# Moving every attention product to VectorE in a hand-ordered two-layer kernel, with more filler matmuls and the order laid anew

## The chip, the cores and the metric

The kernel runs on one core of a Trainium2 chip. The metric is the device time of one execution in microseconds (us). Before the change three runs took 551.32, 551.1 and 556.45 us, with a median of 551.32.

## The reference, cut to what is computed

The input is x (4 batches x 512 positions x 128 channels) and a context of 77 keys per batch. All arithmetic is fp32. Four residual blocks follow one another:

```python
x = x + xattn0(layernorm(x), ctx, ctx, mask, Wq, bq, Wk, bk, Wv, bv, Wo, bo)    # 16 heads x 8, 77 keys, softmax
x = x + ffn0(layernorm(x), ...)
#   ffn0: y1 = LN(z + mha(z))      sequence axis = the 4 batches, 4 heads x 32: scores are 4x4 for each position and head
#         y2 = LN(y1 + moe(y1))    top-1 of 8 experts, each (y1 @ w1 + b1) @ w2 + b2, at most 256 tokens each, times the gate
x = x + xattn1(layernorm(x), ctx)  # q = z Wq^T, k = ctx Wk^T, v = ctx, 16 heads x 8
#         cutoff = the 32nd largest of the 77 scores; scores below it are left out; softmax over the rest
x = x + mix(layernorm(x))          # sigmoid(xr W_r) * (relu(xk W_k)^2 W_v), xr and xk mix each position with the one before it
```

The expert layers have no nonlinearity between w1 and w2, so the kernel multiplies the two weights once at the start.

## The kernel before, in words

**Tiles.** The 2048 positions are 16 tiles of 128 positions (partitions) by 128 channels, t = 4b + j for batch b and quarter j. The first cross-attention (`attend`) runs in four groups j of four tiles; `s0@2` is its score step for b = 0 in group 2. The small attention over the batches (`among`) needs the four tiles of one j together and also runs once for each j. The expert layer, the second cross-attention and the channel mix run tile by tile, t = 0 to 15.

**The order of the work.** Each step of a stage is one token, name@index, in a table ORDER that is written out by hand. Each engine walks the table from front to back and issues those steps that it has a function for (`run`); what order it keeps is that of the table, and semaphores alone tie the engines together. A token such as `norm@3` may stand for a piece on one engine, and the pieces of a tile's chain stand apart in the table with other tiles' work between them. Some wait values are counted from the table (`begun`), so they follow a new order by themselves.

**The first cross-attention.** TensorE makes the scores of 16 heads (s0 to s3, L1070 and L1073), VectorE takes the maximum (mx, L726) and subtracts it (sub, L731), ScalarE exponentiates (exp), TensorE turns the weights (ta, tb, tc), ScalarE copies them (ca, cb, cc, L516 among them), TensorE multiplies with the values (v0 to v3, L1102, 20 matmuls or 10 of two passes), VectorE normalises (nm), TensorE turns and projects (ot, op, L1113), and VectorE adds the residual (x0 to x3, L747). The merging of the expert weights (wa0 to wa7, wt, wu) is TensorE work put among the steps of groups 0 and 1.

**The attention over the batches.** VectorE stores q, k and v (qs, L814). Four products follow, one for each query batch l: qk{l} multiplies q of l with the k of all four (128x512). dot{l} sums them (L845), soft, mexp (L556 on ScalarE) and softw make the softmax, four weighted products wv{l} multiply the values with the weights, and tot{l} sums them (L871). Before the change VectorE makes qk0, qk1 (L821) and wv0, wv1, wv2 (L830); POOL makes qk2, qk3 (L369) and wv3 (L378). The constants QKG = 2 and WVG = 3 set that split, and POOL signals by semaphores of its own:

```python
if l < QKG:
    hold(e, s["m_prod"], QKG * j + l + 1)
else:
    hold(e, s["m_prodg"], (B - QKG) * j + l - QKG + 1)
```

POOL also adds biases (zbias L345, xbias L350), copies the gates (L407), makes the scalars of the layer norms (L395, L397, L399), applies their affine part (L411, L415) and, for each tile of the second attention, makes the difference to the maximum (dif, L430), the difference to the cutoff (cut, L437) and the masked weights (product, p, L444).

**The expert layer.** For each tile: turn and copy, then three matmul steps moe0 to moe2 (L1239), each followed by ScalarE's gated copies (gated0 to gated2: L595, then eight of L598, 3, 4 and 1), then a sum of nine on TensorE (total, L1247), and the layer norm (sum2, square2 L574, scale2 on POOL, norm2 L579, affine on POOL, and sum3 to norm3 again). `cap` is POOL's step that prepares the gates of one group, which the expert tiles of a later j need.

**The second cross-attention.** lturn, lT, ask, qT and scores make the 16 x 77 scores in PSUM; keep (ScalarE, L626) copies them to SBUF; VectorE then finds the 32nd largest by four rounds of maxima of eight (max{round}{head group}, L959) with three rounds of marking the found ones (mark, L967) between them. The 16 tiles follow each other on VectorE without an end, 16 heads x 7 steps each. exp (L634) and sign (L638, L640) on ScalarE and product on POOL make the weights; turn0 to turn2 (L1283) with copy0 to copy2 (L648 to L652) turn them; value (L1299, 20 matmuls) multiplies with the context; norm (VectorE, L992 and L995) normalises. The last tile, 15, is split up by head groups (part0 to part3) and value0 to value2. Then come the channel mix of that tile: fturn, shift, up, acts, down (L1326), fvalue, half and end, and the store.

**Fillers.** `fill@k` is two bf16 matmuls of 128x308 into the half of the turning PSUM that the channel mix also uses (psT[:, 1], L1331); nobody reads the result. They stand where TensorE would otherwise idle. `stoke@k` is the same into the last bank of the score PSUM, free once the last scores are copied. Before the change there are 157 fills and 10 stokes; each of the stokes also waits for a step of the last tile's top-k:

```python
def after():
    hold(e, s["S_kept"], NT)
    hold(e, s["topk_step"], TOPK_STEPS * NT - (STOKES - (k - FILLS)) + 1)
    stream(psS[:, G - 1])
```

## Time and profile before

| what | value |
|---|---|
| runs | 551.32, 551.1, 556.45 us (median 551.32) |
| the profiled execution | 555.6 us |
| its span, first to last instruction | 553.8 us |
| TensorE's mean granted clock in it | 0.88 of full speed |
| VectorE busy | 481.4 us |
| TensorE busy (matmul) | 431.9 us |
| ScalarE busy | 291.3 us |
| GpSimd (POOL) busy | 277.4 us |

All durations below come from the one profiled execution, which took 4.3 us more than the median of the runs. The span is what the trace covers; 1.8 us of the execution lie outside it. Busy shares are means over stages of different kinds: to about 75 us cross-attention with TensorE full, to about 300 us a mixture of all stages, then tile after tile of top-k. Which engine or wait ends a stretch is read from the stretch.

In the rows PE is TensorE's matmul and PEld its weight load, DVE is VectorE, ACT is ScalarE, POOL is GpSimd. Bracketed at a row's end is the time that the engine stood idle before it, and what ended that.

### The profile page before, as it was taken

The numbers are of one execution on the slowest core, as the hardware profiler recorded it, in microseconds if no ns is written. First come the engines' busy times: TensorE is split into PE (matmuls) and PEld (weight loads), VectorE is DVE, ScalarE is ACT, GpSimd is POOL, SyncE is SP. The second block draws the span as 40 slices with busy tenths as digits, with TensorE's granted clock in tenths as the row PEclk, the third lists the DMA queues.
The fourth block names the chain that finished last, engine by engine and source line by source line (L and its number), as shares of the span: only waits on it lengthen the run. The fifth ranks groups of instructions, "written<-read, shape, count | busy, mean of one in ns | idle before, by whom it ended". The sixth has DMA issues, their size and how long they took to land. (4 is left out here: it accounts for less than half of the span.)

```text
span 553.8 us, 10801 instructions
## 1 busy us (share of the span) xinstructions
PE 431.9 (78%) x2655; PEld 325.0 (59%) x2655; DVE 481.4 (87%) x3014; ACT 291.3 (53%) x797; POOL 277.4 (50%) x400
## 2 busy tenths in 40 slices
PE   4989997797896886878977987877876976765285
PEld 4569865566655663656655655655654754553274
DVE  4954679959868798999899999999999999999971
ACT  1225551323443435424877688787777687544333
POOL 4410141504327447535575578668648567554612
PEclk9999998978996999899989899878778889556768
DMA  9600000000000000000000000000000000000000
GB/s 279 290 1 1 2 1 1 1 2 0 2 2 0 2 2 0 2 0 2 7 6 2 5 2 2 11 1 1 11 1 7 1 7 6 2 10 2 5 5 11
DMA packets 5933, 9.60 MB, mean 17 GB/s; under 512 B 744, under 2 KB 4976, under 8 KB 5616
## 3 DMA queue, kind: packets, MB, share of 16 engines
q1 hardware_dynamic: 5584, 8.35, 4.3%
q10 hardware_dynamic: 288, 0.56, 0.3%
q8 instruction: 23, 0.38, 0.3%
q14 instruction: 38, 0.31, 0.2%
HBM read 7.86 MB, written 1.05 MB: 16 GB/s over the span
## 5 line engine op out<-in xcount | busy, mean ns | idle before, releaser
L959 DVE MAX8 top<-area_b 128x8 f32<-128x77 f32 x768 | 112.8, 222 | 0.0
L967 DVE MATCH_REPLACE8 area_b<-top,area_b 128x77 f32<-128x77 f32 x512 | 106.9, 222 | 0.0
L1283 PE MATMUL psT<-consts,p 128*128 128x128 f32 (+1 forms) x160 | 35.1, 348 | 33.8 <-POOL p L444 27.0
L1331 PE MATMUL psT<-mrow,mones 128*128 128x308 bf16 x314 | 53.3, 309 | 1.4 <-ACT pT L516 0.8
L967 DVE MATCH_REPLACE8 area_b<-top,area_a 128x77 f32<-128x77 f32 x256 | 53.5, 223 | 0.0
L1299 PE MATMUL psM<-vblk,pT 128*128 128x135 f32 (+3 forms) x320 | 48.8, 316 | 3.2 <-ACT pT L652 2.6
L1299 PEld LDWEIGHTS psM<-vblk,pT 128*128 128x128 f32 (+1 forms) x320 | 46.5, 225 | 7.6 <-issue 7.2
L1102 PE MATMUL psM<-vblk,pT 128*128 128x135 f32 (+3 forms) x320 | 44.2, 296 | 7.8 <-ACT early L579 4.5
L1283 PEld LDWEIGHTS psT<-consts,p 128*128 128x128 f32 (+1 forms) x160 | 23.1, 174 | 44.4 <-POOL p L444 29.4
L1102 PEld LDWEIGHTS psM<-vblk,pT 128*128 128x128 f32 (+1 forms) x320 | 41.4, 204 | 11.3 <-issue 9.8
L598 ACT ACTIVATE mparts<-psM,cur 128x128 f32<-128x128 f32 x128 | 38.1, 368 | 9.4 <-PE psM L1239 9.3
L444 POOL TENSOR_TENSOR p<-area_b 128x1232 f32<-128x1232 f32 x15 | 41.8, 2787 | 2.0 <-ACT area_b L640 0.9
L1331 PEld LDWEIGHTS psT<-mrow,mones 128*128 128x128 bf16 x314 | 31.8, 103 | 17.9 <-issue 8.5
L959 DVE MAX8 top<-area_a 128x8 f32<-128x77 f32 x256 | 37.5, 223 | 3.6 <-ACT area_a L626 3.6
L967 DVE MATCH_VALUE_LOAD area_b<-top,area_b 128x8 f32 x512 | 40.6, 79 | 0.0
L1247 PE MATMUL psM<-mparts,consts 128*128 128x128 f32 x288 | 39.9, 300 | 0.0
L1247 PEld LDWEIGHTS psM<-mparts,consts 128*128 128x128 f32 x288 | 38.7, 217 | 0.0
L437 POOL TENSOR_TENSOR area_b<-area_a,top 128x1232 f32<-128x1232 f32 x15 | 34.0, 2266 | 9.3 <-DVE top L959 9.2
L430 POOL TENSOR_TENSOR dif<-area_a,top 128x1232 f32<-128x1232 f32 x16 | 36.3, 2268 | 4.1 <-DVE top L959 4.1
L1239 PE MATMUL psM<-w,y1T 128*128 128x512 f32 (+1 forms) x64 | 26.6, 498 | 12.9 <-ACT mparts L598 12.7
L726 DVE TENSOR_REDUCE mx<-psS 128x16 f32<-128x1232 f32 x16 | 23.0, 1439 | 11.7 <-PE psS L1073 11.7
L320 POOL TENSOR_TENSOR rstd_m<-veps_m,expo 128x4 f32<-128x4 f32 x8 | 8.1, 1018 | 42.8 <-DVE veps_m L699 42.7
(224 smaller groups left out, 1050.6 us busy)
## 6 DMA issues: line engine op xcount, KB each, us to landing
area_a<-in_w1T SPq DMA_DIRECT2D x1, 2064.0 KB, 11.2
area_b<-in_w SPq DMA_DIRECT2D x1, 2048.0 KB, 15.5
x<-in_x SPq DMA_DIRECT2D x4, 256.0 KB, 6.9
out<-fin SPq DMA_DIRECT2D x16, 64.0 KB, 1.6
rows<-in_rows SPq DMA_DIRECT2D x1, 576.0 KB, 7.0
vblk<-in_vblk SPq DMA_DIRECT2D x1, 540.0 KB, 15.9
weights<-in_weights SPq DMA_DIRECT2D x1, 516.0 KB, 6.7
consts<-in_consts ACTq DMA_DIRECT2D x1, 392.5 KB, 4.0
```

Source lines behind the costliest of these rows:

```text
L430: e.tensor_tensor(dif[:], scores_sb[t % RING][:], top[:, t % 2, 0, :, 0, None].broadcast_to([P, H, KEYS]), ALU.subtract)\
L437: e.tensor_tensor(cut, scores_sb[t % RING][:], top[:, t % 2, TOPK // 8 - 1, :, 7, None].broadcast_to([P, H, KEYS]), ALU.subtract)\
L444: e.tensor_tensor(p1.rearrange("p (h k) -> p h k", k=KEYS), ex1, cut, ALU.mult).then_inc(s["p_set"], 1)
L598: ins = e.activation(mparts[:, x_], psM0[:, at + (x_ - lo) * D:at + (x_ - lo + 1) * D], ACT.Copy, scale=cur[:, D + x_:D + x_ + 1])
L959: ins = e.max(tops[:, r, h], (left if r else scores_sb[t % RING])[:, h])
L967: ins = e.match_replace(left[:, h], tops[:, r, h], (left if r else scores_sb[t % RING])[:, h], GONE)
L1102: ins = mm(streams(psM0, c), pT[0:w, c], vblk0[0:w, b, c, None, :].broadcast_to([w, copies(c)[0], VB]), start=(c == 0), stop=(c == NCH - 1 ...
L1239: mm(psM0[:, 0:(hi - lo) * D], y1T[:], w12[:, lo:hi].rearrange("p e n -> p (e n)"), start=True, stop=True)\
L1247: ins = mm(psM0[:, 0:D], ident, mparts[:, x_], start=False, stop=(x_ == E))
L1283: ins = tr(psT[0:w, 0, (c % 4) * P:(c % 4 + 1) * P], p1[:, c * P:c * P + w], ident)
L1299: ins = mm(streams(psM1, c), pT1[0:w, c], vblk1[0:w, t // NJ, c, None, :].broadcast_to([w, copies(c)[0], VB]), start=(c == 0), stop=(c == ...
L1331: mm(bank[:, 0:B * KEYS], mones[:], mrow.rearrange("p b k -> p (b k)"), start=True, stop=True)
```

## The change

**Products.** QKG, WVG and the semaphores m_prodg and m_pvg go. POOL loses its product() and weighed(); VectorE makes all 16 q.k products and all 16 weighted products. In the whole program that moves eight q.k products and four weighted ones.

**Fillers.** FILLS goes from 157 to 199 and STOKES from 10 to 60. A stoke no longer waits for a step of the last tile's top-k, only for the last scores to be copied. The first ones now stand right after the last keep, in the top-k of tile 13; none is left in the tail.

**Order.** The table ORDER is laid anew from front to back. Line numbers after the change are 25 lower on POOL, ScalarE and VectorE (2 lower in POOL's part ahead of the removed functions, L318 to L360) and 35 lower on TensorE.

```diff
-QKG = 2
-WVG = 3
-FILLS = 157
-STOKES = 10
+FILLS = 199
+STOKES = 60
...
-                def product(l):
-                    def f():
-                        hold(e, s["q_stored"], B * j + B)
-                        hold(e, s["m_o"], B * j)
-                        e.tensor_tensor(prod[:, l].rearrange("p (m n) -> p m n", m=B),
-                                        qkv[:, l, None, 0:D].broadcast_to([P, B, D]),
-                                        qkv[:, :, D:2 * D], ALU.mult).then_inc(s["m_prodg"], 1)
-                    return f
...
-                for b in range(QKG, B):
-                    steps[f"qk{b}"] = product(b)
-                for b in range(WVG, B):
-                    steps[f"wv{b}"] = weighed(b)
                 return steps
...
                         if b == 0:
-                            hold(e, s["m_pv"], WVG * j)
-                            hold(e, s["m_pvg"], (B - WVG) * j)
+                            hold(e, s["m_pv"], B * j)
...
-                        if l < QKG:
-                            hold(e, s["m_prod"], QKG * j + l + 1)
-                        else:
-                            hold(e, s["m_prodg"], (B - QKG) * j + l - QKG + 1)
+                        hold(e, s["m_prod"], B * j + l + 1)
...
-                        if l < WVG:
-                            hold(e, s["m_pv"], WVG * j + l + 1)
-                        else:
-                            hold(e, s["m_pvg"], (B - WVG) * j + l - WVG + 1)
+                        hold(e, s["m_pv"], B * j + l + 1)
...
-                    if b < QKG:
-                        steps[f"qk{b}"] = product(b)
-                    if b < WVG:
-                        steps[f"wv{b}"] = weighed(b)
+                    steps[f"qk{b}"] = product(b)
+                    steps[f"wv{b}"] = weighed(b)
...
                 def after():
                     hold(e, s["S_kept"], NT)
-                    hold(e, s["topk_step"], TOPK_STEPS * NT - (STOKES - (k - FILLS)) + 1)
+
                     stream(psS[:, G - 1])
...
-total@0 qs3@2 qk0@2 qk1@2 qk2@2 dot0@2 qk3@2 dot1@2 sum2@0 dot2@2 square2@0 load@1 dot3@2 scale2@0 soft@2 mexp@2 norm2@0 softw@2
...
+sum2@0 load@1 dot2@2 square2@0 dot3@2 scale2@0 soft@2 norm2@0 mexp@2 affine@0 v1@3 softw@2 wv0@2 sum3@0 square3@0 wv1@2 scale3@0
```

Three places of the new order follow, each as the engine's own instructions in a row.

POOL before, around the third group's products and the layer norm of expert tile 0 (prod is the attention product, lvar, lrs and lnm are the norm's scalars, cur the gates of the tile):

```order
L345 TENSOR_TENSOR zob<-zt,rows 128x512
L350 TENSOR_TENSOR x<-x,rows 128x128 x4
L369 TENSOR_TENSOR prod<-qkv 128x512 x2
L407 COPY cur<-yg 128x136
L395 TENSOR_SCALAR lvar<-lsq 128x1
L397 TENSOR_TENSOR lrs<-lvar,expo 128x1
L399 TENSOR_TENSOR lnm<-lneg,lrs 128x1
```

POOL after, at the same place:

```order
L348 TENSOR_TENSOR x<-x,rows 128x128 x4
L343 TENSOR_TENSOR zob<-zt,rows 128x512
L382 COPY cur<-yg 128x136
L370 TENSOR_SCALAR lvar<-lsq 128x1
L372 TENSOR_TENSOR lrs<-lvar,expo 128x1
L374 TENSOR_TENSOR lnm<-lneg,lrs 128x1
```

The two products are gone, and the two bias steps have changed places; the scalars of the norm stand behind the copy of the gates alone.

On ScalarE at that place the softmax exponent of the third group (sce) and the normalised tile (early) stand like this before:

```order
L570 ACTIVATE junk,lneg<-psM 128x128
L574 ACTIVATE junk,lsq<-psM,lneg 128x128
L556 ACTIVATE sce<-sc 128x64
L579 ACTIVATE early<-psM,lnm,lrs 128x128
L570 ACTIVATE junk,lneg<-x 128x128
```

and after:

```order
L545 ACTIVATE junk,lneg<-psM 128x128
L549 ACTIVATE junk,lsq<-psM,lneg 128x128
L554 ACTIVATE early<-psM,lnm,lrs 128x128
L531 ACTIVATE sce<-sc 128x64
L545 ACTIVATE junk,lneg<-x 128x128
```

The normalisation now stands ahead of the exponent.

ScalarE before, from the gathering of expert tile 3 to the sum of its layer norm (mparts are the gated copies; area_b<-area_b is sign@1, the top-k weights of tile 1):

```order
L595 ACTIVATE mparts<-psM 128x128
L598 ACTIVATE mparts<-psM,cur 128x128 x3
L638 ACTIVATE area_b<-area_b,tiny 128x1232
L640 ACTIVATE area_b<-area_b 128x1232
L598 ACTIVATE mparts<-psM,cur 128x128 x4
L570 ACTIVATE junk,lneg<-x 128x128
L598 ACTIVATE mparts<-psM,cur 128x128
```

and after:

```order
L570 ACTIVATE mparts<-psM 128x128
L573 ACTIVATE mparts<-psM,cur 128x128 x8
L613 ACTIVATE area_b<-area_b,tiny 128x1232
L615 ACTIVATE area_b<-area_b 128x1232
L545 ACTIVATE junk,lneg<-x 128x128
```

All eight gated copies stand ahead of the two instructions of sign@1 now; before, five of them stood behind.

TensorE before, from the last projection of tile 13's channel mix to that of tile 14's turning (L1299 is value@14, then value0@15 and so on; L1283 turns the weights; L1331 are the stokes):

```order
L1326 MATMUL psT<-weights,ka 128x128
L1299 MATMUL psM<-vblk,pT 128x3x27 x2
L1299 MATMUL psM<-vblk,pT 128x4x27 x2
L1299 MATMUL psM<-vblk,pT 128x5x27 x6
L1331 MATMUL psS<-mrow,mones 128x308 x16
L1283 MATMUL psT<-consts,p 128x128 x4
L1331 MATMUL psS<-mrow,mones 128x308 x2
L1299 MATMUL psM<-vblk,pT 128x3x27 x2
L1299 MATMUL psM<-vblk,pT 128x4x27 x2
L1283 MATMUL psT<-consts,p 128x128 x4
L1331 MATMUL psS<-mrow,mones 128x308 x2
```

TensorE after, from value@12 to value@13, where the new stokes stand (L1264 is value, L1248 the turns, L1296 the stokes):

```order
L1264 MATMUL psM<-vblk,pT 128x5x27 x6
L1291 MATMUL psT<-weights,ka 128x128
L1296 MATMUL psS<-mrow,mones 128x308 x74
L1248 MATMUL psT<-consts,p 128x128 x9
L1248 MATMUL psT<-consts,p 80x128
L1279 MATMUL psT<-consts,zf 128x128
L1264 MATMUL psM<-vblk,pT 128x3x27 x2
L1264 MATMUL psM<-vblk,pT 128x4x27 x2
L1264 MATMUL psM<-vblk,pT 128x5x27 x6
```

and from value@14 to the first two parts of tile 15's values:

```order
L1264 MATMUL psM<-vblk,pT 128x3x27 x2
L1264 MATMUL psM<-vblk,pT 128x4x27 x2
L1264 MATMUL psM<-vblk,pT 128x5x27 x6
L1291 MATMUL psT<-weights,ka 128x128
L1248 MATMUL psT<-consts,p 128x128 x4
L1264 MATMUL psM<-vblk,pT 128x3x27 x2
L1264 MATMUL psM<-vblk,pT 128x4x27 x2
```

Before, 16 stoke matmuls stand between value@14 and turn0@15, and two more each behind turn0@15 and turn1@15. After, 74 stoke matmuls stand ahead of turn0@13, none behind it, and down@13 (L1291) stands behind value@14.

## Rows read from the trace of the kernel before

**Rows 1.** The page, part 1: busy time, share of the span, instructions of each engine.

```profile
PE 431.9 (78%) x2655; PEld 325.0 (59%) x2655; DVE 481.4 (87%) x3014; ACT 291.3 (53%) x797; POOL 277.4 (50%) x400
```

**Rows 2.** Stretches: length, busy us (instructions) of PE, PEld, DVE, ACT, POOL, clock.

```profile
300.00:514.00 214.00, 160.53 (x895) 122.08 (x894) 212.70 (x1779) 150.33 (x437) 139.44 (x211) 0.81 0.02 4
480.00:500.00 20.00, 13.38 (x57) 10.48 (x56) 20.00 (x169) 11.09 (x25) 12.59 (x14) 0.52 0.02 7
```

**Rows 3.** Waits of VectorE: who waits, for whom: us in all, times, longest.

```profile
DVE rden L992 <- PE psM L1299: 9.5, 4, 5.1
...
DVE x L747 <- PE psM L1113: 5.0, 3, 2.8
...
DVE top L959 <- ACT area_a L626: 3.6, 4, 2.4
...
DVE oo L871 <- POOL prod L378: 0.6, 1, 0.6
...
DVE sc L845 <- POOL prod L369: 0.5, 1, 0.5
```

**Rows 4.** VectorE's products: group (busy, mean ns), then source line (min/median/max ns).

```profile
L830 DVE TENSOR_TENSOR prod<-qkv,sc 128x512 f32<-128x512 f32 x12 | 16.5, 1414 | 0.1
L821 DVE TENSOR_TENSOR prod<-qkv 128x512 f32<-128x512 f32 x8 | 8.4, 1090 | 0.1
...
L821 DVE TENSOR_TENSOR prod<-qkv x8: 684/693/1762, 80.1 to 215.4; 128x512 f32<-128x512 f32 x8
...
L830 DVE TENSOR_TENSOR prod<-qkv,sc x12: 1037/1074/2836, 87.0 to 224.7; 128x512 f32<-128x512 f32 x12
```

**Rows 5.** Timeline, 166 to 184 us: start us, busy us, engine, what.

```profile
166.14 3.44 POOL L369 TENSOR_TENSOR prod<-qkv 128x512 f32<-128x512 f32 x2 [7.56 <-DVE qkv L814]
...
168.48 0.19 ACT L574 ACTIVATION_READ_ACCUMULATOR junk<-psM,lneg 128x1 f32 x1
...
169.90 0.19 POOL L395 TENSOR_SCALAR lvar<-lsq 128x1 f32<-128x1 f32 x1
...
171.58 0.44 ACT L579 ACTIVATE early<-psM,lnm,lrs 128x128 f32<-128x128 f32 x1
...
172.27 4.75 PE L1102 MATMUL psM<-vblk,pT 128*128 128x81 f32 x20 [4.50 <-ACT early L579]
...
182.30 0.29 DVE L747 TENSOR_TENSOR x<-psM,x 128x128 f32<-128x128 f32 x1 [2.77 <-PE psM L1113]
...
182.98 2.34 DVE L959 MAX8 top<-area_a 128x8 f32<-128x77 f32 x16 [0.39 <-ACT area_a L626]
```

**Rows 6.** Timeline, 256 to 279 us: expert tile 3 and the scores it leads to.

```profile
256.31 1.12 PE L1239 MATMUL psM<-w,y1T 128*128 128x512 f32 x2 [0.15 <-ACT mparts L598]
...
257.62 1.32 ACT L638 ACTIVATE area_b<-area_b,tiny 128x1232 f32<-128x1232 f32 x1 [1.36 <-POOL area_b L437]
...
260.11 1.13 ACT L598 ACTIVATE mparts<-psM,cur 128x128 f32<-128x128 f32 x4
...
277.45 2.34 DVE L959 MAX8 top<-area_a 128x8 f32<-128x77 f32 x16 [2.39 <-ACT area_a L626]
```

**Rows 7.** Timeline, 36 to 95 us: a score step and two value steps.

```profile
36.81 0.80 PE L1070 MATMUL psS<-kblk,hT 32*128 32x308 f32 x8 [2.23 <-DVE d L731]
...
81.80 2.55 PE L1102 MATMUL psM<-vblk,pT 128*128 128x81 f32 x20 [0.16 <-issue]
...
91.51 3.31 PE L1102 MATMUL psM<-vblk,pT 128*128 128x81 f32 x20 [1.83 <-DVE x L747]
```

**Rows 8.** Timeline, 503 to 537 us: turn0@14, tile 15's first maxima, stokes, norm@14.

```profile
503.89 1.12 PE L1283 MATMUL psT<-consts,p 128*128 128x128 f32 x4 [4.85 <-POOL p L444]
...
512.34 2.31 DVE L959 MAX8 top<-area_a 128x8 f32<-128x77 f32 x16
...
536.18 2.57 PE L1331 MATMUL psS<-mrow,mones 128*128 128x308 bf16 x16
...
536.43 0.26 DVE L992 RECIPROCAL rden<-psM 128x16 f32<-128x16 f32 x1 [3.35 <-PE psM L1299]
```

More of the change, by code:

```diff
@@ new lines @@
+acts@6 max23@8 half@6 norm3@10 mark20@8 value@7 gated0@11 mark21@8 mark22@8 mark23@8 lturn@10 down@6 moe1@11 lT@10 fvalue@6 max30@8
+end@6 max31@8 ask@10 gated1@11 max32@8 max33@8 qT@10 scores@10 max00@9 cut@8 max01@9 moe2@11 keep@10 max02@9 max03@9 gated2@11
+norm@7 keys@11 sign@8 total@11 mark00@9 dif@9 mark01@9 mark02@9 load@12 sum2@11 mark03@9 product@8 square2@11 max10@9 max11@9
+max12@9 max13@9 scale2@11 exp@9 turn0@8 mark10@9 mark11@9 add3@7 norm2@11 sum4@7 affine@11 turn@12 mark12@9 square4@7 copy@12
@@ new lines @@
+max31@10 norm2@13 keys@13 max32@10 keep@12 affine@13 max33@10 max00@11 cut@10 sum3@13 max01@11 up@8 square3@13 max02@11 turn@14
+max03@11 copy@14 mark00@11 acts@8 dif@11 moe0@14 sign@10 mark01@11 down@8 mark02@11 mark03@11 scale3@13 gated0@14 max10@11
+product@10 norm@9 norm3@13 moe1@14 max11@11 fvalue@8 max12@11 lturn@13 gated1@14 max13@11 mark10@11 half@8 lT@13 moe2@14 add3@9
+exp@11 ask@13 end@8 mark11@11 turn0@10 qT@13 mark12@11 gated2@14 scores@13 sum4@9 square4@9 mark13@11 keep@13 total@14 scale4@9
```

247 lines of the change are left out of this document (118 added, 129 removed).

## The prediction

> **What bounds the kernel now.** I began with the page's busy times [rows 1]: VectorE works 481.4 of 553.8 us, 87%, more than any other engine. That is an average, so the view by stretches came next [rows 2]: from 300 to 514 us VectorE is busy 212.70 of 214 us, while TensorE is busy 160.53 of them and its granted clock is only 0.81. The top-k rounds, all VectorE's, bound that stretch; whatever another engine gains there buys nothing. The end can move through three things only: VectorE's own work, the 72.4 us (553.8 less 481.4) in which it idles, and the tail. The waits of VectorE say where to look [rows 3]: 5.0 us for x L747, 9.5 us for the attention sums (rden L992, four times), 3.6 us for kept scores before a maximum (top L959, four times), and a last 1.1 us for products that POOL was still making.
>
> **The products.** Twelve instructions move from POOL to VectorE: eight q.k products and four weighted values. Undisturbed, VectorE's take 0.69 and 1.07 us (medians, [rows 4]). List price: 8 x 0.69 + 4 x 1.07 = 9.8 us. But the eight q.k products already on VectorE take 8.4 us where 8 x 0.69 = 5.5 would do, and the twelve weighted ones 16.5 instead of 12.8 [rows 4]: their longest, 1.76 and 2.84 us, ran beside a POOL product. With no such product on POOL, 2.9 + 3.7 us come back, and the 1.1 us of waiting goes [rows 3]. Net: 9.8 - 2.9 - 3.7 - 1.1 = +2.1 us, about 0.5 for each of the four groups j. The third group lies beside a wait of 2.8 us (below), so I book **+1.6**. Bounds: if other POOL work slows the moved ones as much as the mean shows and nothing comes back, 8 x 1.09 + 4 x 1.41 = 14.4 us; if every product is undisturbed, the waits go and half of the remainder lies beside TensorE's latencies, +1.
>
> The GPSIMD Engine Reference of the Trainium skill (Key points) says that GpSimd and VectorE share their SBUF interfaces and collide when a Vector instruction has two SBUF inputs. The trace agrees: 0.69 us against 1.76 for the same shape. By the rule the sum holds; without it the product term would be 9.8 us instead of 1.6.
>
> **The first top-k.** POOL's two q.k products of the third group run 166.14 to 169.58 us, and only then come the scalars of expert tile 0's layer norm (L395 at 169.90), although ACT had read out the sum of squares by 168.7. ACT then puts the softmax exponent (L556) ahead of the normalisation (L579), which starts at 171.58; value v1@3 on TensorE waits for that until 172.27 and runs 4.75 us at the lower clock [rows 5]. Through nm1, ot1 and op1 this is the 2.77 us that VectorE waits at x L747, with another 0.39 us for kept scores before its first MAX8 at 182.98. In the change POOL has no products and norm2@0 stands ahead of mexp@2. The scalars can start at 168.7, take 1.1 us, and L579 starts near 170. VectorE's own queue becomes last: from 166.09 four products (2.5), four sums (2.5), the softmax (1.9), four weighted values (4.0), nm1 (0.5), four sums (2.5), x1 (0.3): 180.3, so at most -2.7; I take **-2.5**. Bounds 0 and -3.2.
>
> **Scores of tile 3.** ACT runs the Sign and Relu of the top-k weights (L638, L640: 257.62 to 260.2) ahead of the four gated copies of tile 3 (L598 at 260.11). Their matmul was out at 257.4, so the tile's chain is 2.7 us late, and at its end VectorE stands 2.39 us for the kept scores [rows 6]. The change puts gated1@3 ahead of sign@1, and cap@3, where the chain starts, one marking round and two maxima earlier. The 2.39 us go: **-2.4**. Fillers in that chain rise from 21 to 25, 8 matmuls or 1.3 us at 0.16 [rows 8], less than the room won. The other small waits (of the 9.5 us on rden L992 3.35 and 5.10 belong to the tail, which leaves 1.1; of the 3.6 us on top L959 0.39 and 2.39 are spoken of, which leaves 0.8) I put at **-0.5** together; bounds -2 and +2, since the changed order can make such waits as well as end them.
>
> **The front.** To 75 us TensorE is nearly full and sets the pace. Between scores s0@0 and s0@1 it stands 2.2 us for a subtraction [rows 7] and runs 17 fillers; the change moves v0@0 and v1@0 into that space and the weight merging (wa0 to wa7) behind them, with 13 fillers there and one ahead of s0@0. Laid out by hand with the same durations, s0@1 comes about 1 us earlier with ot1, op1, tb2 and tc2, some 1.4 us of matmuls, already behind it. I take **-2.0**, from +1 to -4.
>
> **The second group's v3.** Five fillers now stand before v3@1 and the clock still falls: v3@1 takes 3.31 us where v2@1 takes 2.55 [rows 7]. Fourteen stand there in the change. If the full clock holds, **-0.8**; bounds 0 and -1.2.
>
> **The tail.** Today VectorE finishes part1@15 at 533.1 and stands 3.35 us at norm@14 until value@14 ends at 536.4; then 16 filler matmuls (2.57 us) hold turn0@15, which has everything it needs, and four more such matmuls stand among the last turns [rows 8]. All these go, and down@13 moves behind value@14. That takes up to 3 us off the chain. In exchange the last matmuls may run at the lower clock: the fillers were there to keep it up. The 20 matmuls of a value step alone take 2.55 us at one level and 4.75 at the other [rows 5, 7]; with the turns and the last projections I estimate 3.5 us for the whole end at the lower level. I take **-1.0**, between -3 and +2. The fillers are put earlier: 37 stokes, 74 matmuls, stand ahead of turn0@13. At 2.57 us for 16 [rows 8] they take 12 us; TensorE has 4.85 us free there today. But the 23 stokes before them should have brought the clock up, so value@12 and value@13 take some 2.6 us each [rows 7] instead of 4.75 [rows 5]. So turn0@13, today at 503.9, comes 12 - 4.85 - 2.1 = 5 us late; its turns and copies take 5 us and value@13 2.6, to about 516.5. VectorE wants it at norm@13, now after max00@15, at 512.9 [rows 8]: it stands some 3 us, and that fits into the 3.35 us it stands later anyway. Booked at nothing; if that cover is gone it costs 3 us.
>
> TensorE: Matmul & The Clock Gate of the Trainium skill (Part 1) says that idling takes the array to 1.2 GHz and that activity releases it. The 4.75 us of v1@3 after a 4.5 us idle, and the 2.55 of a v behind steady work, agree: if the fillers held nothing, the -0.8 above would be 0.
>
> **Sum.** 1.6 - 2.5 - 2.4 - 0.5 - 2.0 - 0.8 - 1.0 = -7.6 us. The profiled execution took 555.6 us (span 553.8, 1.8 around it), so it would take 548.0. That execution stands 4.3 us over the median of the runs, 551.32 (551.1 to 556.45): the same program has a faster course, in which some waits that I remove may be shorter. The whole sum off the median gives 543.7; I say **544.0**.
>
> **Rivals.** *The order gives back what it wins (within 1%).* 42 more fillers are 84 matmuls, 13.5 us of TensorE time at 0.16 each [rows 8], and most stand in front of steps that VectorE will want; norm@0, norm@1 and norm@13 are asked for 1.2 to 1.7 us of top-k work earlier, norm@12 even 6.2 us. For it: VectorE already waits 9.5 us on rden L992. Against it: between 300 and 514 us TensorE has 53 us free (214 less 160.5). If the front wins nothing (+2.0) and new waits eat 2.4 us elsewhere, -3.2 is left: 548.1 us.
>
> *The stokes stop the tail (slower).* Place: the 74 matmuls ahead of turn0@13. If the clock is at its lower level through them, they take 24 us instead of 12, turn0@13 comes near 523, 19 us late, norm@13 stops VectorE at the start of tile 15 by about as much, and 3.35 us of it are covered: +15.7. With the other terms (-6.6): +9.1, 560.4 us. It decides from about 15 us for the 74: then turn0@13 is 10 us late, and the 6.7 us that are not covered eat the other terms. For it: from 480 to 500 us, where the first stokes will run, the granted clock is 0.52 today [rows 2]. Against it: TensorE is busy only 13.38 of those 20 us, 23 stokes will fill the rest ahead of the 74 matmuls, and the 16 filler matmuls that follow the steady work of value@14 run at the full clock [rows 8].
>
> *The move costs its list price.* Optimise the most contended engine first, says Perfetto Trace Analysis of the Trainium skill (Identifying the Most-Contended Engine); work put on it then lengthens the kernel one for one. Here that is VectorE. As a mechanism of this kernel: the 6.6 us of slowed products do not come back, because L350, L411 and L415 collide with them instead. Then the products cost 9.8 instead of 1.6 us: 552.2 us.
>
> **Chances.** Forecast (gain of 5 to 11 us) 0.53; order gives back 0.28; list price 0.07; stokes stop the tail 0.12. Measured beside a before that itself spreads over 5 us, 1% (5.5 us) is about what can be told from no change. Faster by over 1%, below 545.8: most of the forecast and a little of the first rival, 0.53. Slower by over 1%: 0.12. Within: 0.35. The unknown terms together span +4 to -13 around the sum, not all at one end; the range 537.5 to 552.5 leaves out the slower rival's core and the far end of the gains.
>
> **What would show it.** Right: VectorE's busy time rises by 2 to 4 us only, and every q.k product takes 0.69 us; no Vector wait on POOL's products; the first MAX8 comes 4 to 5 us earlier; no 2.39 us gap at tile 3; norm@13 waits 3 us or less; the 74 stokes take about 12 us. Wrong: products still at 1.1 and 1.4 us on the mean; new waits on rden L992 or kept scores that sum to more than 5 us; a half clock through the stokes; more from the end of value@14 to the end of the span than today's 17.4 us (553.8 less 536.4).

## The result and the profile after

The changed kernel takes 563.28 us (median of 4 runs, 556.81 to 563.55) against 551.21 us for the kernel before (median of 4, 551.1 to 556.45). The ratio is 1.0175 with a 95% interval of 1.0116 to 1.0233: slower by 1.75%, where 544.0 us and a gain were forecast. The profiled execution took 563.55 us, with a span of 561.7. Medians here and below are of all executions of a kernel, while the ratios use only those within 1.5% of its fastest.

The page of the changed kernel, its busy times, answers to [rows 1], and below it stand its chain that ended last and VectorE's largest waits (who waits for whom: us in all, times, longest), which answer to [rows 3]. The lines have moved: VectorE's L959 is L924 now, its L992 is L957 and x L747 is L722.

```profile
PE 449.1 (80%) x2839; PEld 336.1 (60%) x2839; DVE 482.8 (86%) x3026; ACT 292.2 (52%) x797; POOL 257.2 (46%) x388
...
PE 40%; DVE 33%; ACT 11%; issue 8%; POOL 5%; DMA 1%; SPq 0%; ACTq 0%; DVEq 0%; POOLq 0%
```

```profile
DVE rden L957 <- PE psM L1264: 24.1, 7, 5.6
DVE mx L701 <- PE psS L1038: 16.4, 9, 6.2
...
DVE top L924 <- ACT area_a L601: 2.9, 2, 2.2
DVE x L722 <- PE psM L1078: 1.8, 3, 1.2
```

VectorE's work grew by 1.4 us only (482.8 against 481.4). The largest loss is one wait: VectorE stands 24.1 us for weighted values (rden, the step norm), where it was 9.5. Its wait for scores before mx grew as well, from 11.7 to 16.4 us, but that is in the first attention, which ends earlier than before all the same. Of the chain that ended last 40% lie on TensorE and 33% on VectorE, though VectorE is the busier engine.

To see where, I take the first maximum of a tile as a mark. First the kernel before (tiles 7, 10 and 14; tiles 0 and 3 stand in [rows 5] and [rows 6]), then the changed one (tiles 0, 3, 7, 10, 14), both from VectorE's timeline.

```profile
356.25 1.76 DVE L959 MAX8 top<-area_a 128x8 f32<-128x77 f32 x12
...
414.51 2.32 DVE L959 MAX8 top<-area_a 128x8 f32<-128x77 f32 x16
...
492.91 2.33 DVE L959 MAX8 top<-area_a 128x8 f32<-128x77 f32 x16
```

```profile
177.76 2.34 DVE L924 MAX8 top<-area_a 128x8 f32<-128x77 f32 x16 [2.22 <-ACT area_a L601]
...
270.22 2.34 DVE L924 MAX8 top<-area_a 128x8 f32<-128x77 f32 x16
...
352.41 2.35 DVE L924 MAX8 top<-area_a 128x8 f32<-128x77 f32 x16
...
416.67 2.34 DVE L924 MAX8 top<-area_a 128x8 f32<-128x77 f32 x16
...
503.43 2.33 DVE L924 MAX8 top<-area_a 128x8 f32<-128x77 f32 x16
```

| stretch | before | after | difference |
|---|---|---|---|
| start to first maximum (tile 0) | 182.98 | 177.76 | -5.2 |
| tile 0 to tile 3 | 94.5 | 92.5 | -2.0 |
| tile 3 to tile 7 | 78.8 | 82.2 | +3.4 |
| tile 7 to tile 10 | 58.3 | 64.3 | +6.0 |
| tile 10 to tile 14 | 78.4 | 86.8 | +8.4 |
| tile 14 to the end of the span | 60.9 | 58.3 | -2.6 |

The ends gain 9.8 us, the middle loses 17.8. In the middle the prediction had no term but -0.5. The waits of VectorE there, from VectorE's timeline of the changed kernel at norm@2, norm@6, norm@7 and norm@11:

```profile
291.52 0.26 DVE L957 RECIPROCAL rden<-psM 128x16 f32<-128x16 f32 x1 [3.95 <-PE psM L1264]
...
379.77 0.26 DVE L957 RECIPROCAL rden<-psM 128x16 f32<-128x16 f32 x1 [3.93 <-PE psM L1264]
...
399.49 0.26 DVE L957 RECIPROCAL rden<-psM 128x16 f32<-128x16 f32 x1 [1.86 <-PE psM L1264]
...
487.90 0.26 DVE L957 RECIPROCAL rden<-psM 128x16 f32<-128x16 f32 x1 [5.28 <-PE psM L1264]
```

With 2.91 and 0.59 us at norm@8 and norm@9 these make 18.5 us between 277 and 503 us; before it was 1.1.

**How a value comes to be late: tile 8.** The timeline of the changed kernel:

```profile
395.49 3.96 PE L1264 MATMUL psM<-vblk,pT 128*128 128x81 f32 x20
...
399.40 0.38 PE L1291 MATMUL psT<-weights,ka 128*128 128x128 f32 x2
...
399.60 0.28 ACT L588 ACTIVATE early<-psS 128x128 f32<-128x128 f32 x1 [2.76 <-PE psS L1220]
...
400.25 0.46 POOL L444 TENSOR_TENSOR vv<-vv,er 128x128 f32<-128x128 f32 x1 [5.99 <-ACT vv L657]
...
401.19 2.27 POOL L412 TENSOR_TENSOR area_b<-area_a,top 128x1232 f32<-128x1232 f32 x1
...
404.44 1.32 ACT L613 ACTIVATE area_b<-area_b,tiny 128x1232 f32<-128x1232 f32 x1
...
407.24 0.30 POOL L382 COPY cur<-yg 128x136 f32<-128x136 f32 x1 [1.17 <-PE psM L1212]
...
407.49 2.78 POOL L419 TENSOR_TENSOR p<-area_b 128x1232 f32<-128x1232 f32 x1
...
410.33 0.66 PE L1248 MATMUL psT<-consts,p 128*128 128x128 f32 x4 [3.23 <-POOL p L419]
```

and that of the kernel before:

```profile
391.73 0.64 PE L1326 MATMUL psT<-weights,ka 128*128 128x128 f32 x2
...
394.13 2.49 PE L1299 MATMUL psM<-vblk,pT 128*128 128x81 f32 x20
...
395.33 2.27 POOL L437 TENSOR_TENSOR area_b<-area_a,top 128x1232 f32<-128x1232 f32 x1 [0.68 <-DVE top L959]
...
397.63 1.32 ACT L638 ACTIVATE area_b<-area_b,tiny 128x1232 f32<-128x1232 f32 x1 [0.16 <-POOL area_b L437]
...
400.35 2.78 POOL L444 TENSOR_TENSOR p<-area_b 128x1232 f32<-128x1232 f32 x1
```

In both, VectorE finds the last maximum of tile 8 at about 395 us. Before, POOL takes cut@8 at once (395.33) and product@8 follows at 400.35. After, value@7 runs at the lower clock (3.96 us instead of 2.49) and ahead of down@6 (399.40 instead of 391.73); POOL stands 5.99 us for tile 6's channel mix, cut@8 starts at 401.19, sign@8 waits on ScalarE behind the last gated copy of tile 11 until 404.44, and product@8 starts at 407.49. TensorE then stands 3.23 us for it, and norm@8 comes 2.91 us late. Four engines in fixed order hand the delay round. Two more places of the new order lie in this chain. On ScalarE the copy vv for tile 6's channel mix (fvalue@6, L657) now stands behind lT@10 (L588), which waits 2.76 us for a matmul (L1220) that stands behind value@7 on TensorE; before, fvalue@6 stood ahead of it. And on POOL load@12 (L382), which waits for tile 11's expert sum (L1212), now stands ahead of product@8; before, it stood behind. That is a reading of one trace; which part of it is a cause is for the experiments.

### The profile page after: what moved, and what is told of

Same layout as the page of the kernel before. It is cut to its first block, busy times and chain, and to the rows that moved or that the text cites. A ratio compares the mean times of both kernels' runs of the same rounds, so it can differ in the third digit from the quotient of the medians.

```text
span 561.7 us, 11202 instructions
## 1 busy us (share of the span) xinstructions
PE 449.1 (80%) x2839; PEld 336.1 (60%) x2839; DVE 482.8 (86%) x3026; ACT 292.2 (52%) x797; POOL 257.2 (46%) x388
## 4 chain that ended last, share of the span: by engine, by line
PE 40%; DVE 33%; ACT 11%; issue 8%; POOL 5%; DMA 1%; SPq 0%; ACTq 0%; DVEq 0%; POOLq 0%
DVE area_b L932 11%; DVE top L924 10%; PE psM L1067 5%; PE psM L1264 5%; PE psM L1212 3%; PE psM L1204 3%; ACT mparts L573 3%; PE psT L1056 2%; PE psM L1199 2%; PE psT L1296 2%; PE psS L1035 2%; PE psM L1140 2%; PE psS L1038 2%; PE psT L1248 2%; ACT area_b L613 2%
## 5 line engine op out<-in xcount | busy, mean ns | idle before, releaser
L924 DVE MAX8 top<-area_b 128x8 f32<-128x77 f32 x768 | 113.0, 231 | 0.0
L1296 PE MATMUL psT<-mrow,mones 128*128 128x308 bf16 x398 | 65.7, 307 | 2.8 <-DVE vblk L751 2.2
L1296 PEld LDWEIGHTS psT<-mrow,mones 128*128 128x128 bf16 x398 | 40.1, 102 | 21.7 <-issue 6.1
L1248 PE MATMUL psT<-consts,p 128*128 128x128 f32 (+1 forms) x160 | 32.9, 330 | 24.0 <-POOL p L419 16.9
L1264 PE MATMUL psM<-vblk,pT 128*128 128x135 f32 (+3 forms) x320 | 46.8, 306 | 3.5 <-ACT pT L627 2.2
L1264 PEld LDWEIGHTS psM<-vblk,pT 128*128 128x128 f32 (+1 forms) x320 | 44.6, 216 | 7.9 <-issue 7.5
L1067 PE MATMUL psM<-vblk,pT 128*128 128x135 f32 (+3 forms) x320 | 42.6, 290 | 6.2 <-ACT early L554 2.8
L1067 PEld LDWEIGHTS psM<-vblk,pT 128*128 128x128 f32 (+1 forms) x320 | 40.4, 200 | 9.2 <-issue 7.2
L932 DVE MATCH_VALUE_LOAD area_b<-top,area_b 128x8 f32 x512 | 45.2, 88 | 0.0
L318 POOL TENSOR_TENSOR rstd_m<-veps_m,expo 128x4 f32<-128x4 f32 x8 | 8.1, 1018 | 78.9 <-DVE veps_m L674 78.8
L1248 PEld LDWEIGHTS psT<-consts,p 128*128 128x128 f32 (+1 forms) x160 | 22.2, 167 | 34.4 <-POOL p L419 19.1
L1212 PE MATMUL psM<-mparts,consts 128*128 128x128 f32 x288 | 41.3, 307 | 0.0
L1204 PE MATMUL psM<-w,y1T 128*128 128x512 f32 (+1 forms) x64 | 29.2, 543 | 14.1 <-ACT mparts L573 14.1
L924 DVE MAX8 top<-area_a 128x8 f32<-128x77 f32 x256 | 37.7, 233 | 2.9 <-ACT area_a L601 2.9
L1212 PEld LDWEIGHTS psM<-mparts,consts 128*128 128x128 f32 x288 | 40.0, 223 | 0.0
L412 POOL TENSOR_TENSOR area_b<-area_a,top 128x1232 f32<-128x1232 f32 x15 | 34.0, 2265 | 8.4 <-DVE top L924 8.4
L701 DVE TENSOR_REDUCE mx<-psS 128x16 f32<-128x1232 f32 x16 | 23.0, 1438 | 16.5 <-PE psS L1038 16.4
```

What stands on the lines that cost most here:

```text
L412: e.tensor_tensor(cut, scores_sb[t % RING][:], top[:, t % 2, TOPK // 8 - 1, :, 7, None].broadcast_to([P, H, KEYS]), ALU.subtract)\
L924: ins = e.max(tops[:, r, h], (left if r else scores_sb[t % RING])[:, h])
L932: ins = e.match_replace(left[:, h], tops[:, r, h], (left if r else scores_sb[t % RING])[:, h], GONE)
L1067: ins = mm(streams(psM0, c), pT[0:w, c], vblk0[0:w, b, c, None, :].broadcast_to([w, copies(c)[0], VB]), start=(c == 0), stop=(c == NCH - 1 ...
L1204: mm(psM0[:, 0:(hi - lo) * D], y1T[:], w12[:, lo:hi].rearrange("p e n -> p (e n)"), start=True, stop=True)\
L1212: ins = mm(psM0[:, 0:D], ident, mparts[:, x_], start=False, stop=(x_ == E))
```

## The experiments

Every kernel below was run with a profile and timed in 3 rounds (e7 and e8 in 5) beside the kernel before on the same chip. Several splice the two tables: "the change to X, before to Y, the change" means the steps of the change's order up to token X, then those of before's order that have not been done, up to Y, then the rest as the change has them; fillers and stokes come with the piece that they stand in.

**e1, the products alone.**

```diff
-QKG = 2
-WVG = 3
+QKG = 4
+WVG = 4
```

> The kernel before with all 32 products of the attention over the batches on VectorE and nothing else changed. Theory (the products are cheap, what was lost lies in the order): VectorE's busy time rises by 1 to 3 us, q.k products of 0.69 us each, time 551 to 555 us. Rival (the moved products cost their list price of 9.8 us, and the order only hid part of it): 558 to 562 us.

Measured: 553.61 us against 552.15, ratio 1.0003 (0.9965 to 1.0041). VectorE's products, by form (busy us, mean ns), in e1 and, second, in the change:

```profile
L830 DVE TENSOR_TENSOR prod<-qkv,sc 128x512 f32<-128x512 f32 x16 | 16.7, 1094 | 0.1
L821 DVE TENSOR_TENSOR prod<-qkv 128x512 f32<-128x512 f32 x16 | 10.3, 685 | 0.1
```

```profile
L804 DVE TENSOR_TENSOR prod<-qkv,sc 128x512 f32<-128x512 f32 x16 | 16.3, 1072 | 0.1
L795 DVE TENSOR_TENSOR prod<-qkv 128x512 f32<-128x512 f32 x16 | 11.0, 745 | 0.1
```

VectorE's products take 2.1 us more for twelve more of them (27.0 against 24.9, [rows 4]), not 9.8, its busy time as a whole is 481.1 us against 481.4, and the time shows nothing. The move isn't the cause.

**e2, the order alone.** The change with QKG = 2, WVG = 3 and POOL's products kept.

> The order, the 199 fillers and the 60 stokes of the change, with the twelve products left on POOL. Theory (the order loses the time): 560 to 564 us, with waits of VectorE for weighted values of over 15 us in all, as in the change. Rival (the products on VectorE are what makes it late): 551 to 554 us.

Measured: 564.83 us, ratio 1.0232 (1.0165 to 1.0299); VectorE waits 25.4 us at rden. The time is near the theory's 560 to 564 and far from the rival's: the order with its fillers is the cause.

**e3, the front of the change, the rest of before.**

```diff
-ORDER = the change
+ORDER = the change to max00@3, then before
```

> The changed kernel up to the first maximum of tile 3, and from there the order of before with its fillers and its 10 stokes behind their old wait. Theory (the first part gains 7 us that the second part's order gives back): first maximum of tile 3 at 270 us, no wait for weighted values over 2 us before tile 14, time 543 to 546 us. Rival (VectorE that comes 7 us earlier finds TensorE late under any order, since the chain to the weighted values hangs on TensorE and its clock): the waits come back, 549 to 555 us.

Measured: 551.65 us, ratio 0.9997 (0.9968 to 1.0026). My theory (543 to 546 us) failed and the rival's range held. The front's gain is there (first maximum of tile 3 at 271.7 us, before 277.45), but 4.2 of these 5.8 us are handed back: VectorE now waits 3.64 us at norm@2, and tile 3 to tile 7 takes 83.0 us instead of 78.8. Tiles 7 to 14 take 136.6, as before (136.7). In this kernel, and in e8 below (83.0 us for the same four tiles, 3.68 us at norm@2), before's order could not use the lead. Whether that is the order's doing or the clock's is not shown: in both, TensorE's granted clock was down to 0.66 from 272 to 277 us, ahead of that wait, and in the kernel before it was 1.00 there. What the change's order loses from tile 7 on comes on top.

**e4, one suspected step.** In the trace of the change TensorE stands 2.36 us at turn@10, with turn1@6 behind it. Moved, and the same for tile 7 with turn@11 and copy@11:

```diff
-turn@10 copy0@6 max20@7 copy@10 turn1@6 scale4@5 max21@7 sum3@9 moe0@10 copy1@6 max22@7 norm4@5 turn2@6
+copy0@6 max20@7 turn1@6 turn@10 scale4@5 max21@7 sum3@9 copy1@6 copy@10 max22@7 norm4@5 turn2@6 moe0@10
```

> The changed kernel with turn@10 and turn@11 (and copy@10, copy@11, moe0@10) put behind the second turning of tiles 6 and 7, as before. Theory (turn@10 waits 2.4 us for a layer norm and holds the turning of tile 6 behind it, and the late norm@6 carries on to tiles 7 to 9): the wait of 3.93 us at norm@6 falls below 1.5 and those of tiles 7 to 9 with it, 555 to 559 us. Rival (the half clock in that stretch makes the values late, whatever stands ahead of them): the waits stay, 561 to 565 us.

Measured: 568.3 us, ratio 1.0298 (1.0235 to 1.036), norm@6 waits 4.66 us. Wrong: value@6 starts 25.4 us behind tile 7's first maximum instead of 24.1, and the scores of tile 12 come 92.7 us behind it instead of 90.1.

**e5, fewer fillers.** FILLS from 199 to 133, the 66 from fill@133 on taken out.

> The changed kernel without its fillers 133 to 198 (132 matmuls, from the end of tile 1's top-k to tile 5's). Theory (fillers load TensorE in front of the expert chain): 21 us of TensorE work fall away, the expert totals of tiles 4 to 8 come earlier, 555 to 560 us. Rival (the fillers hold the clock, without them more of the real matmuls run at half speed): 565 to 572 us, and the stretches at half clock between 250 and 400 us more than double from today's 37 us.

Measured: 570.63 us, ratio 1.0254 (1.0201 to 1.0306), beside the change's 1.0116 to 1.0233: no gain, a loss if anything. The stretch of 200 us in which they stood, without them and, second, with them (length, busy us of PE, PEld, DVE, ACT, POOL, then clock):

```profile
200.00:400.00 200.00, 154.88 (x867) 113.53 (x867) 187.66 (x1426) 124.21 (x372) 117.91 (x175) 0.83 0.01 4
```

```profile
200.00:400.00 200.00, 166.61 (x1008) 121.59 (x1007) 187.37 (x1423) 123.41 (x371) 117.22 (x177) 0.89 0.01 3
```

TensorE is less busy, at a lower clock, and VectorE does as much in either. The fillers did not load TensorE to any harm; from tile 7 to the end it is 212.7 us, without a filler between there and tile 13 in either kernel. The median lies in the rival's range, but its number did not come as stated: 0.89 and 0.83 of 200 us are 44 and 68 us at half the clock, not twice as much.

**e6, values in one piece.** For tiles 6 to 11: turn0, copy0, turn1, copy1, turn2, copy2 and value behind one another.

> The changed kernel with the turnings, copies and value step of tiles 6 to 11 put in one piece right behind turn0, ahead of the expert steps that stood among them. Theory (the weighted values ride behind the expert chain on TensorE, and VectorE that runs ahead of that chain waits for them): the waits at norm@6 to norm@11, 14.6 us today, fall below 4, time 551 to 556 us. Rival (the work is only moved: the expert chain comes later in turn, and VectorE waits for scores or for the next values instead): 560 to 566 us.

Measured: 596.35 us, ratio 1.0798 (1.0763 to 1.0833), the largest loss of all. The waits at norm@6 to norm@11 are 32.4 us. Now TensorE stands 0.6 to 0.8 us at each copy of a tile with nothing behind it that it may do, the scores of tile 12 are made at 466.6 us instead of 442.5, and the wait moves to tiles 9 and 11 (11.1 and 11.7 us). Weaving the chains is what keeps TensorE going; the theory that the values only had to be taken out of the weave is wrong.

**e7, the tail of the change behind before's order.** Before to max00@13 with all products on VectorE, then the change.

> The kernel before up to the first maximum of tile 13, with all products on VectorE, and from there the order of the change with its 60 stokes. Theory (the tail of the change is a gain of its own): 548 to 550.5 us, no wait at norm@13 over 2 us, value@12 to value@14 at 2.6 us each. Rival (the stokes stop turn0@13, and the gain was seen only because VectorE came late): 552 to 556 us with a wait of 3 us or more at norm@13.

Measured: 554.34 us, ratio 1.0023 (0.9996 to 1.005). From tile 14 to the end: 59.2 us; but e1, with the old tail, has 58.6 where before had 60.9. The tail of the change gains nothing that can be told from that spread, and the theory's 548 to 550.5 us did not come. No wait at norm@13 over 0.52 us: the 37 stokes do not stop anything here either.

**e8, three pieces.** The change to max00@3, before to max00@13, the change.

> Three pieces: the order of the change up to the first maximum of tile 3, that of before up to the first maximum of tile 13, that of the change from there. Theory (the middle of the change is what loses, and the tail's gain adds to whatever the front leaves): 546.5 to 549.5 us. Rival (each piece's gain is given back by the next wait): 551 to 554 us.

Measured: 550.9 us, ratio 0.9978 (0.9956 to 1.0). Between the theory's range and the rival's, as e3 and e7 let expect.

**e9, before's order for tiles 7 to 12 only.** No filler stands in this stretch in either order, so FILLS and STOKES stay as the change has them.

```diff
-ORDER = the change
+ORDER = the change to max00@7, before to max00@13, the change
```

> The changed kernel with the order of before from the first maximum of tile 7 to that of tile 13 (no filler stands in either order there). Theory (the order of that stretch is what makes the values of tiles 6 to 11 late, whatever lead VectorE has): the waits at norm@6 to norm@11 (14.6 us in the change) fall below 3, time 550 to 553 us. Rival (they come from VectorE's lead or from what tiles 3 to 6 left behind on TensorE): they stay over 8 us, 557 to 563 us.

Measured: 549.28 us, ratio 0.994 (0.9907 to 0.9973). VectorE's wait for values in the whole profile, which was 24.1:

```profile
DVE rden L957 <- PE psM L1264: 7.4, 5, 4.9
```

Tile 7 to the end takes 195.5 us, in the change 209.3: 13.8 us lie in the order of six tiles. This kernel beats both, the one before by 0.6%. The mean clock does not explain the loss of this stretch: from tile 7 to tile 10 the granted clock was 0.79 before, 0.78 in the change and 0.80 here, and from tile 10 to tile 14, where the change takes 86.8 us and the kernel before 78.4, it was 0.85 in the change and only 0.78 before.

**e10, the reverse.** All products on VectorE, before to max00@7, then the change.

> All products on VectorE, the order and fillers of before up to the first maximum of tile 7, and from there the order of the change with its 60 stokes. Theory (the order from tile 7 on loses by itself): waits at norm@6 to norm@11 of 8 to 15 us in all, 561 to 567 us. Rival (the lead of 4 us that VectorE brings along makes the waits, and here it has none): under 5 us of waits, 551 to 554 us.

Measured: 568.83 us, ratio 1.0302 (1.0243 to 1.0361). With e1 as its like (194.6 us from tile 7 to the end, here 208.6) the order of these tiles costs 14.0 us, and VectorE brought no lead. The rival is out. Over all profiles, the stretch from tile 7 to the end takes 194.6 to 197.6 us in the six with before's order of tiles 7 to 12 (before, e1, e3, e7, e8, e9) and 208.6 to 212.7 in the four with the change's order there (the change, e2, e5, e10). Within one order it moves by 3 to 4 us, and so less than that is not told by one profile.

**e11, more fillers ahead of the turnings.** Eight more fills ahead of turn0 of tiles 6 to 11.

> The changed kernel with eight more fillers (16 matmuls) right ahead of turn0 of each of the tiles 6 to 11, where TensorE waits for POOL's product. Theory (values at half clock are late because TensorE idles ahead of their turnings): the value steps of tiles 6, 7 and 11 fall from 3.3, 4.0 and 4.2 us to 2.5, 557 to 561 us. Rival (the fillers delay the turnings by their own 2.6 us each, and the clock falls elsewhere): 565 to 572 us.

Measured: 562.5 us, ratio 1.0189 (1.0123 to 1.0255), as the change. Value@6 fell to 2.48 us and value@11 to 2.55, both at a granted clock of 1.00, value@7 rose to 4.45 at 0.53; tile 7 to the end 212.0. The clock was held at one step and lost at the next.

**e12, two steps of tile 8's delay undone.** acts@6, half@6, down@6 ahead of value@7, sign@8 behind cut@8.

> The changed kernel with acts@6, half@6 and down@6 put ahead of value@7, as before, and sign@8 on ScalarE right behind cut@8, ahead of keep@10 and gated2@11. Theory (down@6 behind value@7 holds POOL's fvalue part and with it cut@8 for 5.5 us, and sign@8 waits behind the gated copy on top): product@8 comes 5 us earlier, at most 7 us behind the last maximum of tile 8, norm@8 waits under 1 us instead of 2.9, 558 to 561 us. Rival (what is moved ahead pushes the expert chain back, and another norm waits instead): 562 to 566 us.

Measured: 571.24 us (561.71 to 573.02), ratio 1.0239 (1.0126 to 1.0352): no gain, and no loss that is told from the change's 1.0116 to 1.0233. The profiled execution is the one of 573.02 us. In it product@8 starts 17.3 us behind tile 8's last maximum instead of 12.1, norm@8 waits 7.46. ScalarE, put to wait at sign@8, held up gated2@11 behind it, tile 11's expert sum came late, and POOL stood for that sum at load@12, right ahead of product@8:

```profile
415.11 0.30 POOL L382 COPY cur<-yg 128x136 f32<-128x136 f32 x1 [6.17 <-PE psM L1212]
```

**e15 and e16, halves of the stretch.** The change with before's order from max00@7 to max00@10 (e15), and from max00@10 to max00@13 (e16).

> The changed kernel with the order of before from the first maximum of tile 7 to that of tile 10 only. Theory (the first late values, those of tiles 6 to 8, start the loss and each later one follows from it): 551 to 555 us, since tiles 10 to 13 then start on time. Rival (each tile's order loses its own 2 to 5 us): about half of the 14 us between the change and the whole exchange comes back, 555 to 559 us, with the wait of 5 to 6 us at norm@11 still there.

> The changed kernel with the order of before from the first maximum of tile 10 to that of tile 13 only. Theory (the loss starts in tiles 7 to 9): waits at norm@6 to norm@8 of about 9 us as in the change, and little else comes back, 558 to 562 us. Rival (each tile's order loses its own): 554 to 558 us, no wait at norm@11.

Measured: e15 555.14 us over ten runs, four of 542.6 to 550.7 and six of 555.1 to 556.3 us, ratio 0.9892 (0.9838 to 0.9945). The profiled execution took 556.27 us, so I go by the stretch alone: 199.0 us from tile 7 to the end, 10.3 less than the change. e16: 560.88 us, ratio 1.0122 (1.0025 to 1.0218), 206.5 us, 2.8 less. In e15 the wait at norm@11 is 2.71 us, in e16 it is gone, but norm@8 and norm@9 wait 4.50 and 4.33. And e16's 2.8 us do not lie where its order was exchanged: tile 7 to tile 10, in the change's order, takes 61.3 us instead of 64.3, tile 10 to tile 14, in before's, 86.7 where the change has 86.8. So the loss begins in tiles 7 to 9 and is handed on: from tile 10 to tile 14 the change takes 86.8 us, e9 77.7, and e15, whose order is the change's there, 80.5. Of those 9.1 us 6.3 were inherited, as far as three single profiles tell.

**e17 and e18, single tiles; e19, two TensorE steps.** Before's order for tile 7 alone, for tile 8 alone; and this:

```diff
-moe0@11 acts@6 max23@8 half@6 norm3@10 mark20@8 value@7
+moe0@11 acts@6 max23@8 half@6 norm3@10 mark20@8 down@6 moe1@11 value@7
```

> The changed kernel with the order of before from the first maximum of tile 7 to that of tile 8 only. From the first maximum of tile 7 to the end the change takes 209.3 us, with tiles 7 to 9 exchanged 199.0. Theory (the first late value, norm@6, starts it): 200 to 203 us for that stretch. Rival (each tile adds its own): 206 to 208 us.

> The changed kernel with the order of before from the first maximum of tile 8 to that of tile 9 only. Theory (value@7 ahead of down@6 and moe1@11 is the costly step, since product@8 then waits for both): product@8 within 8 us of tile 8's last maximum instead of 12, and 201 to 204 us from the first maximum of tile 7 to the end. Rival (tile 7's order started it): 206 to 209 us.

> The changed kernel with two steps on TensorE moved: down@6 and moe1@11 ahead of value@7, as before. Theory (these two behind value@7 hold cut@8 on POOL and, through the gated copies ahead of sign@8 on ScalarE, product@8): product@8 within 8 us of tile 8's last maximum, norm@8 waits under 1 us, 202 to 205 us from the first maximum of tile 7 to the end. Rival (no single step does it, value@7 behind two more steps is late itself): norm@7 waits 2 us more than the 1.9 of the change, 208 to 211 us.

Measured: e17 559.52 us, ratio 1.0125 (1.0075 to 1.0175), 205.8 us from tile 7 to the end (-3.5). e18 557.39 us, ratio 1.0045 (0.9999 to 1.0091), 202.5 us (-6.8), with product@8 10.5 us behind the last maximum. e19 564.13 us, ratio 1.0207 (1.0152 to 1.0262), 211.2 us: norm@7 waits 5.25 us, product@8 comes 14.8 us behind. Tile 8's order is the largest piece that was found. That tile 7's adds to it is not shown, since 3.5 us is within what one order moves by. The two steps that I had named do not carry the loss by themselves, and the trace of e19 says why:

```profile
393.03 0.63 PE L1291 MATMUL psT<-weights,ka 128*128 128x128 f32 x2
...
400.55 0.28 ACT L588 ACTIVATE early<-psS 128x128 f32<-128x128 f32 x1 [6.16 <-PE psS L1220]
400.72 0.27 ACT L657 ACTIVATE vv<-psT 128x128 f32<-128x128 f32 x1
```

Down@6 (L1291) was done at 393.7, but ScalarE's copy of it, fvalue@6 (L657), stood behind lT@10 (L588), which waited 6.16 us for a matmul behind value@7. So cut@8 started 9.1 us behind the last maximum. In e12 the same order stood (down@6 at 398.2, its copy at 402.7). In e18, where fvalue@6 stands ahead of value@7 as before, cut@8 started 1.7 us behind the last maximum; what kept product@8 back there was ScalarE's sign@8 behind the copies of keep@10 and gated2@11, and then load@12 on POOL, 1.38 us. No run moved fvalue@6 or load@12 alone.

## The clock, in one and the same order

Tile 3 to tile 7 took 82.1 to 82.2 us in the change, e4, e6, e12, e15, e17 and e18, and 78.6 in e9, e11, e16 and e19, though all of these have the same order up to tile 7. The difference is the wait at norm@2, 3.9 us or 0.4. TensorE's timeline of the change, and of e9 behind it, at the same steps:

```profile
281.64 1.06 PE L1248 MATMUL psT<-consts,p 128*128 128x128 f32 x4
...
283.35 1.65 PE L1199 MATMUL psM<-w,y1T 128*128 128x384 f32 x2
...
285.22 1.75 PE L1296 MATMUL psT<-mrow,mones 128*128 128x308 bf16 x6
286.76 1.91 PE L1204 MATMUL psM<-w,y1T 128*128 128x512 f32 x2
288.47 0.42 PE L1220 MATMUL psS<-consts,early 128*128 128x128 f32 x1
288.68 2.81 PE L1264 MATMUL psM<-vblk,pT 128*128 128x81 f32 x20
```

```profile
283.62 0.66 PE L1248 MATMUL psT<-consts,p 128*128 128x128 f32 x4
...
284.62 0.91 PE L1199 MATMUL psM<-w,y1T 128*128 128x384 f32 x2
...
285.59 0.95 PE L1296 MATMUL psT<-mrow,mones 128*128 128x308 bf16 x6
286.74 1.12 PE L1204 MATMUL psM<-w,y1T 128*128 128x512 f32 x2 [0.20 <-ACT mparts L573]
287.70 0.27 PE L1220 MATMUL psS<-consts,early 128*128 128x128 f32 x1
287.81 2.48 PE L1264 MATMUL psM<-vblk,pT 128*128 128x81 f32 x20
```

Until the clock returns within the value step, the steps of the first take 1.6 to 1.8 times as long. The granted clock of that stretch, in the change from 270 to 290 us and in e9 from 272 to 292:

```profile
270.00:280.00 10.00, 7.66 (x51) 5.49 (x48) 10.00 (x86) 7.88 (x23) 9.15 (x10) 0.96 0.01 2
280.00:290.00 10.00, 9.33 (x32) 6.06 (x33) 7.57 (x65) 5.70 (x23) 3.16 (x9) 0.53 0.02 7
```

```profile
272.00:282.00 10.00, 7.73 (x52) 5.54 (x50) 10.00 (x85) 7.88 (x23) 8.85 (x8) 1.00 0.01 2
282.00:292.00 10.00, 8.40 (x56) 6.00 (x57) 9.59 (x80) 7.28 (x28) 3.93 (x12) 1.00 0.02 7
```

The ten microseconds ahead are alike (7.66 and 7.73 us busy), and yet one kernel runs on at 2.4 GHz and the other falls to 1.2. TensorE: Matmul & The Clock Gate of the Trainium skill (Part 1) ties the fall to idling; with 2.3 us idle in ten in both, these rows do not say what decides it. It costs 3.6 us where it falls on a value that VectorE wants at once, and it is probably one source of the spread that each of these kernels shows: of the change's four runs the fastest, 556.81 us, had a mean granted clock of 0.908, the other three (563.06 to 563.55) 0.891 to 0.900.

## Why the prediction was wrong, point by point

- **Products: +1.6 us predicted, right.** The growth of the products alone that stands behind it was 9.8 - 6.6 = 3.2 us; it measured 2.1 us in e1 and 2.4 in the change, and the list price (9.8 us) was wrong as a rival. Its mechanism exists, but is small: one q.k product of the change took 1.65 us instead of 0.69, beside POOL's cut (L412). VectorE's whole busy time rose by 1.4 us where 2 to 4 were forecast. Perfetto Trace Analysis in the Trainium skill (Identifying the Most-Contended Engine) says to optimise the busiest engine first. The prediction's rival took from it that work put on this engine lengthens the kernel one for one, and in e1 it did not; the order of the queues decided instead.
- **First top-k and front: -2.5 and -2.0 predicted, -5.2 together, right in sum, in part by luck.** x3@0 came 3.6 us earlier (61.87 against 65.50), x1@3 7.0 us earlier (175.26 against 182.30), and then 2.22 us of the gain went into a wait for kept scores ahead of the first MAX8. That mark lay between 174.9 and 181.2 us in the profiles with this front and VectorE's products, 181.8 to 183.0 with before's; in e2, the one with this front and POOL's products, at 182.4. The means are 178.7 and 182.5 us, so the gain at this mark is about 3.8 us and not 5.2, where 4 to 5 were forecast.
- **Scores of tile 3: -2.4 predicted, right.** The gap is gone, and tile 0 to tile 3 is 2.0 us shorter (90.9 to 92.5 us in all profiles with this order, 93.4 to 96.4 with before's).
- **v3@1: -0.8 predicted, right.** It takes 2.55 us.
- **Tail: -1.0 predicted, -2.6 in the profile,** of which e1 has 2.3 without the new tail; so nothing is shown for it. The 74 stoke matmuls took 9.85 us (12 predicted). Turn0@13, forecast 5 us late, started 11.8 us behind tile 14's first maximum where it had been 11.0 (503.89 us in [rows 8] is this step's row and not turn0@14's), and norm@13 waited for nothing. The rival that they stop the tail is out; that its 560.4 us lies nearest to the 563.28 measured is chance.
- **The step that failed** is "the other small waits ... I put at -0.5 together; bounds -2 and +2". They were +17.8 us between tile 3 and tile 14. I had read three places of the new order and took the rest as neutral, because "TensorE has 53 us free" there. That argument is what was wrong: TensorE issues in a fixed order, so time that it stands idle in front of one step is of no use to the step behind. The first rival named the right mechanism (new waits at rden) and sized it at 2.4 us; these waits grew by 14.6 us. The prediction's own sign of being wrong, more than 5 us of new waits on rden, came true.

The sum by what was measured: order of tiles 7 to 12 +13.8 (change against e9), tile 7 to the end otherwise -2.1 (e9 against before, 195.5 and 197.6), tile 2's value at the lower clock +3.6, the rest of tiles 3 to 6 -0.2, front -5.2, tiles 0 to 2 -2.0: +7.9. The spans differ by 7.9 too (561.7 less 553.8); these are single executions, and the medians differ by 12.1.

What stays open: which rule tells a good order of tiles 7 to 12 from a bad one. Of three attempts at single steps (e4, e12, e19) none gained; e4 and the one at a simple rule (e6) made it worse beyond their intervals. The two steps that the traces of e12, e18 and e19 point to, fvalue@6 behind lT@10 on ScalarE and load@12 ahead of product@8 on POOL, were not tried by themselves. And what a steady full clock would give back there wasn't tried, since nothing in the program sets it.

## What to carry to other kernels

When several engines run a hand-laid order, the busiest engine's time is not the bound by itself: look at what the step that it will ask for next has ahead of it in each of the other queues, for every tile of the pattern and not at three places. A relaid order should be exchanged piece by piece against the old one with the first event of a tile as a mark; two splices (e9 and e10) said more here than four repairs of steps that the trace seemed to blame. When a step is moved ahead on one engine, look where its successor stands on the next one: down@6 came 7 us before its copy in e19. And a gain at the front is worth only what the stages behind can take over: in e3 4.2 of 5.8 us were handed back within four tiles.
